# Router logits from raw rows, the last two tiles written out, and an earlier first list in a decoder layer

## The reference

```
x = x + xattn(layernorm(x), ctx)                      # the rows "x2"
xf = layernorm(x).reshape(2048, 256)                  # the rows "xn3"
route_prob = softmax(xf @ Ws + bs, axis=-1).T         # 8 x 2048
route_vals, routes = top_k(route_prob, 256)           # per expert
h   = gelu(xf[routes] @ W1[e] + b1[e])                # 256 x 1024
out = (h @ W2[e] + b2[e]) * route_vals
x   = x + scatter_add(out by routes)
```

## Time and profile before

| what | us |
|---|---|
| median of 3 runs | 368.83 |
| lowest, highest | 368.15, 371.8 |
| the profiled execution | 368.73 |
| its span, first to last instruction | 366.9 |
| TensorE busy | 321.4 (88%) |
| DVE busy | 281.0 (77%) |
| ScalarE busy | 189.2 (52%) |
| POOL busy | 195.0 (53%) |

### The profile page before, as it was taken

One profiled execution on the slowest core, in us unless ns is written; L12 is line 12 of the kernel. 1 busy time (PEld: TensorE's weight loads), 2 busy tenths in 40 slices (PEclk: granted clock), 3 DMA queues, 4 the chain that ended last, 5 costly groups with the idle time before them and its releaser, 6 DMA issues.

```text
span 366.9 us, 6429 instructions
## 1 busy us (share of the span) xinstructions
PE 321.4 (88%) x2346; PEld 289.8 (79%) x2346; DVE 281.0 (77%) x626; ACT 189.2 (52%) x370; POOL 195.0 (53%) x243
## 2 busy tenths in 40 slices
PE   8989998899979999999999982116999999999991
PEld 8867886675559999999999881106999999999991
DVE  2888888848877888888888846777578699689850
ACT  1677654446463467567755642682417556652230
POOL 3778789723142538887888783304314514543222
PEclk9999999999989999999999997555999999999997
DMA  7960000000000136134142346201148657611222
GB/s 234 378 226 1 2 0 2 0 0 3 0 2 0 42 117 188 34 126 136 66 144 79 122 146 185 116 0 31 57 155 249 173 213 189 172 19 41 30 30 29
DMA packets 24047, 34.29 MB, mean 93 GB/s; under 512 B 1784, under 2 KB 20560, under 8 KB 23888
## 3 DMA queue, kind: packets, MB, share of 16 engines
q1 hardware_dynamic: 20112, 29.36, 24.5%
q0 software_dynamic: 3072, 4.20, 6.5%
q10 hardware_dynamic: 832, 0.32, 0.4%
HBM read 27.58 MB, written 6.29 MB: 92 GB/s over the span
## 4 chain that ended last, share of the span: by engine, by line
PE 71%; DVE 13%; POOL 7%; ACT 4%; issue 3%; DMA 1%; DVEq 0%; POOLq 0%; ACTq 0%
PE bank L913 13%; PE bank L915 12%; PE bank L914 12%; PE q_banks L913 4%; PE bank L934 4%; PE q_banks L915 4%; PE q_banks L914 4%; PE bank L769 2%; DVE flags_all L1272 2%; PE q_banks L714 2%; PE bank L732 2%; PE bank L1448 2%; PE bank L748 2%; PE bank L978 1%; POOL acc L406 1%
## 5 line engine op out<-in xcount | busy, mean ns | idle before, releaser
L1573 POOL DMA_INDIRECT out_x<-ybuf,idx x16 | 26.1, 1629 | 59.8 <-DVE ybuf L1593 57.7
L1042 POOL TENSOR_TENSOR prob<-prob,rsum 128x1024 f32<-128x1024 f32 x16 | 30.5, 1906 | 18.8 <-DVE rsum L1140 17.4
L913 PE MATMUL bank<-H_hi,PT_hi 128*128 128x256 f32 x128 | 36.3, 284 | 1.7 <-DVE PT_lo L1111 1.7
L913 PE MATMUL bank<-W_hi,h_hi 128*128 128x256 f32 x128 | 37.2, 291 | 0.0
L915 PE MATMUL bank<-H_hi,PT_lo 128*128 128x256 f32 x128 | 36.2, 283 | 0.0
L915 PE MATMUL bank<-W_hi,h_lo 128*128 128x256 f32 x128 | 36.2, 283 | 0.0
L914 PE MATMUL bank<-H_lo,PT_hi 128*128 128x256 f32 x128 | 36.2, 283 | 0.0
L914 PE MATMUL bank<-W_lo,h_hi 128*128 128x256 f32 x128 | 36.2, 283 | 0.0
L1022 ACT ACTIVATE prob<-prob 128x1024 f32<-128x1024 f32 x16 | 16.9, 1059 | 34.8 <-DVE prob L1161 34.8
L1530 ACT ACTIVATE hbuf<-bank,b_cols 128x256 f32<-128x256 f32 x32 | 13.4, 471 | 40.1 <-PE bank L915 40.1
L1553 POOL DMA_INDIRECT xg<-xn_rows,idx x16 | 18.9, 1180 | 23.7 <-DVE idx L1621 19.4
(11 more groups left out here) (262 smaller groups left out, 1067.3 us busy)
## 6 DMA issues: line engine op xcount, KB each, us to landing
W_raw<-in_L_ffn_W SPq DMA_DIRECT2D x16, 1024.0 KB, 5.7
X<-in_x SPq DMA_DIRECT2D x4, 512.0 KB, 7.1
xn_rows<-xn SPq DMA_DIRECT2D x16, 128.0 KB, 1.8
out_x<-X SPq DMA_DIRECT2D x4, 512.0 KB, 3.6
Wq<-in_L_xattn_Wq SPq DMA_DIRECT2D x1, 1024.0 KB, 11.5
Wk<-in_L_xattn_Wk SPq DMA_DIRECT2D x1, 1024.0 KB, 14.1
Wv<-in_L_xattn_Wv SPq DMA_DIRECT2D x1, 1024.0 KB, 15.5
Wo<-in_L_xattn_Wo SPq DMA_DIRECT2D x1, 1024.0 KB, 16.9
```

The lines of the kernel that those rows point to most:

```text
L913: t.matmul(out_ps, hi, rhs_hi, start=first, stop=False)
L1042: g.tensor_tensor(prob[:, s], prob[:, s], rsum[:, s].unsqueeze(2).to_broadcast([P, HX, CK]), ALU.mult).then_inc(prob_ready, 1)
L1573: g.indirect_dma_start(out_flat, bass.IndirectOffsetOnAxis(ap=idx[:, e, h:h + 1], axis=0), ybuf[:, h], None, bounds_check=last_row, oob_is ...
```

## The change

- The router's logits are made from the transposed rows x2 themselves and from Ws less its columns' means. The means come in part 1: a tile mean_of of 1/256, two matmuls behind the "cols" transposes, a copy by ScalarE, a subtraction by DVE; ws_sb is loaded earlier. x2 of tile k-1 is transposed in step k. The factor rstd3 (now kept for all 16 tiles) is applied to the logits by DVE.
- The loop ends with step 13. The last two tiles are written out for each engine (`pe_drain`, `act_drain`, `pool_drain`, `dve_drain`). Tile 15's probabilities are scaled half by POOL, half by DVE; its product goes to bank 0; xn3 of tiles 14 and 15 is made by POOL; the softmax is taken over the first 14 tiles, in PSUM (`some`, in bank 1), and over each of the last two alone.
- POOL's second weight half of the drain comes last. SP sends the last output rows and loads W2 of expert 3 ahead of the last two xn3 tiles. POOL's iotas wait for the stored xn3 tiles instead of out_full.
- The first list's one-hot is made in three parts, and its list is read ahead of the second one-hot.

```diff
+            g.memset(mean_of[:], 1.0 / D)
             order(g.memset(ident[:], 0.0))
...
+            pe.wait_ge(ld["ws"], 16)
+            for m in range(MC):
+                mm = t.matmul(ps[:, P:P + E], mean_of[:], ws_sb[:, m], start=m == 0, stop=m == MC - 1)
+            filled(mm, "cols")
...
+            dve.wait_ge(cols_ready, 3)
+            v.tensor_tensor(ws_sb[:], ws_sb[:], gate_mean[:].unsqueeze(1).to_broadcast([P, MC, E]),
+                            ALU.subtract).then_inc(gate_ready, 1)
...
-        STEPS = steps(-LEAD_T, NT + DONE)
+        LAST = NT - 1
+        STEPS = steps(-LEAD_T, LAST - 1)
...
+        def x2_transposes(pe, n):
+
+            pe.wait_ge(x2_ready, n + 1)
+            for m in range(MC):
+                mm = nc.tensor.transpose(banks[6][:, D + m * P:D + (m + 1) * P], X[:, n, m * P:(m + 1) * P], ident[:])
+            return mm
...
-                pe.wait_ge(*xn3_of(n))
+            if old.within(NT):
                 if not nxt.within(NT):
                     pe.wait_ge(xT_ready, NT)
-                for m in range(MC):
-                    mm = t.transpose(banks[6][:, D + m * P:D + (m + 1) * P], xn3[:, s, m * P:(m + 1) * P], ident[:])
+                mm = x2_transposes(pe, old.n)
...
+        def pe_drain(pe):
+
+            n = LAST - 1
+            pe.wait_ge(prob_ready, n + 1)
+            pe.wait_ge(PT_ready, 2 * n)
+            prob_transposes(n, 0)
+            prob_transposes(n, 1)
+            pe.wait_ge(xT_ready, NT)
+            x2_transposes(pe, n - 1).then_inc(T_full, 1)
+            logits_product(pe, n - 1)
+            pe.wait_ge(PT_ready, 2 * n + 1)
+            out_product(banks[7], n, range(4))
+            pe.wait_ge(PT_ready, 2 * n + 2)
+            pe.wait_ge(prob_ready, NT)
+            prob_transposes(LAST, 0)
+            pe.wait_ge(last_prob_ready, 1)
+            prob_transposes(LAST, 1)
+            out_product(banks[7], n, range(4, 8)).then_inc(out_full, 1)
+
+            pe.wait_ge(shifted, LAST)
+            pe.wait_ge(PT_ready, 2 * LAST + 1)
+            out_product(banks[0], LAST, range(4))
+            pe.wait_ge(PT_ready, 2 * LAST + 2)
+            x2_transposes(pe, n).then_inc(T_full, 1)
+            out_product(banks[0], LAST, range(4, 8)).then_inc(out_full, 1)
+            pe.wait_ge(shifted, NT)
+            logits_product(pe, n).then_inc(logits_full, 1)
+
+            x2_transposes(pe, LAST).then_inc(T_full, 1)
+            logits_product(pe, LAST).then_inc(logits_full, 1)
...
+        def act_drain(act):
+            a = nc.scalar
+            n = LAST - 1
+            PT_high(act, n)
+            x2T_evac(act, n - 1)
+            for nth in LAST_HALVES:
+                W_high(act, nth)
+            PT_high(act, LAST)
+            xn3_row(act, n - 1)
+            x2T_evac(act, n)
+            act.wait_ge(shifted3, 1)
+            a.activation(some, some, ACT.Exp).then_inc(exp3_ready, 1)
+            x2T_evac(act, LAST)
+            for i in (n, LAST):
+                act.wait_ge(shifted3, i - n + 2)
+                a.activation(logits[:, i], logits[:, i], ACT.Exp, bias=rowmax[:, i:i + 1],
+                             accum_out=rowsum[:, i:i + 1]).then_inc(exp3_ready, 1)
...
+        def row_scale(pool, n, order):
+
+            g = nc.gpsimd
+            s = n % 2
+            pool.wait_ge(var3_ready, n + 1)
+            order(g.tensor_tensor(rstd3[:, n:n + 1], mv3[:, s, 1:2], eps_col[:], ALU.add))
+            raised = g.tensor_tensor(rstd3[:, n:n + 1], rstd3[:, n:n + 1], neg_half[:, 0:1], ALU.pow)
+            raised.then_inc(rstd3_ready, 1)
+            order(g.tensor_tensor(nmean3[:, s:s + 1], mv3[:, s, 0:1], neg_one[:], ALU.mult))
+            pool.wait_ge(rstd3_ready, n + 1)
+            return g.tensor_tensor(nmean3[:, s:s + 1], nmean3[:, s:s + 1], rstd3[:, n:n + 1], ALU.mult)
...
+        def pool_drain(pool, order):
+            g = nc.gpsimd
+            n, s = LAST - 1, LAST % 2
+            pool.wait_ge(rsum_ready, NT)
+            g.tensor_tensor(prob[:, s, 0:HALF], prob[:, s, 0:HALF],
+                            rsum[:, s, 0:HALF].unsqueeze(2).to_broadcast([P, HALF, CK]), ALU.mult).then_inc(prob_ready, 1)
+            row_scale(pool, n - 1, order).then_inc(nmean3_ready, 1)
+            W_low(pool, LAST_HALVES[0])
+            pool.wait_ge(xn3_ready, n)
+            row_scale(pool, n, order).then_inc(nmean3_ready, 1)
+            row_scale(pool, LAST, order).then_inc(nmean3_ready, 1)
+            pool.wait_ge(nmean3_ready, NT)
+            for i in (n, LAST):
+                pool.wait_ge(xn3_stored, 16 * (i - 1) + 16)
+                g.tensor_scalar(xn3[:, i % 2], X[:, i, :], rstd3[:, i:i + 1], nmean3[:, i % 2:i % 2 + 1], ALU.mult,
+                                ALU.add).then_inc(last_xn3_ready, 1)
+            W_low(pool, LAST_HALVES[1])
...
+        def dve_drain(dve, order):
+            v = nc.vector
+            n, s = LAST - 1, LAST % 2
+
+            def row_moments(i):
+                order(v.bn_stats(stats3[:, i % 2], X[:, i, :]))
+                v.bn_aggr(mv3[:, i % 2], stats3[:, i % 2]).then_inc(var3_ready, 1)
+
+            raw_logits = v3(banks[7][:, D:D + (NT - 2) * E], NT - 2)
+            add_out(dve, n - 1, banks[7])
+            dve.wait_ge(exp_ready, NT)
+            order(v.tensor_reduce(sums[:, s], prob[:, s], AX.X, ALU.add))
+            v.reciprocal(rsum[:, s], sums[:, s]).then_inc(rsum_ready, 1)
+            PT_low(dve, n)
+            dve.wait_ge(rsum_ready, NT)
+            v.tensor_tensor(prob[:, s, HALF:], prob[:, s, HALF:], rsum[:, s, HALF:].unsqueeze(2).to_broadcast([P, HALF, CK]),
+                            ALU.mult).then_inc(last_prob_ready, 1)
+            row_moments(n - 1)
+            PT_low(dve, LAST)
+            add_out(dve, n, banks[7])
+            row_moments(n)
+
+            dve.wait_ge(nmean3_ready, n)
+            dve.wait_ge(ld["small"], 32)
+            order(v.tensor_tensor(some, raw_logits, rstd3[:, ROUTED].unsqueeze(2).to_broadcast([P, n, E]), ALU.mult))
+            order(v.tensor_tensor(some, some, bs_bc[:].unsqueeze(1).to_broadcast([P, n, E]), ALU.add))
+            order(v.tensor_reduce(rowmax[:, ROUTED], some, AX.X, ALU.max))
+            v.tensor_tensor(some, some, rowmax[:, ROUTED].unsqueeze(2).to_broadcast([P, n, E]),
+                            ALU.subtract).then_inc(shifted3, 1)
+            add_out(dve, LAST, banks[0])
+            row_moments(LAST)
+            for i in (n, LAST):
+                dve.wait_ge(logits_full, i - n + 1)
+                dve.wait_ge(rstd3_ready, i + 1)
+                order(v.scalar_tensor_tensor(out=logits[:, i], in0=logits_of(i), scalar=rstd3[:, i:i + 1], in1=bs_bc[:],
+                                             op0=ALU.mult, op1=ALU.add))
+                v.tensor_reduce(rowmax[:, i:i + 1], logits[:, i], AX.X, ALU.max, negate=True).then_inc(shifted3, 1)
+                if i == n:
+                    dve.wait_ge(exp3_ready, 1)
+                    order(v.tensor_reduce(rowsum[:, ROUTED], some, AX.X, ALU.add))
+                    order(v.reciprocal(rowsum[:, ROUTED], rowsum[:, ROUTED]))
+                    v.tensor_tensor(probs[:, :, ROUTED].rearrange("p e i -> p i e"), some,
+                                    rowsum[:, ROUTED].unsqueeze(2).to_broadcast([P, n, E]), ALU.mult)
+                dve.wait_ge(exp3_ready, i - n + 2)
+                order(v.reciprocal(rowsum[:, i:i + 1], rowsum[:, i:i + 1]))
+                ins = v.tensor_scalar(probs[:, :, i], logits[:, i], rowsum[:, i:i + 1], None, ALU.mult)
+            ins.then_inc(probs_ready, 1)
...
+            def rows_out(n):
+                sp.wait_ge(x2_ready, n + 1)
+                sp.dma_start(out_rows[:, n - NJ + 1:n + 1, :], X[:, n - NJ + 1:n + 1, :]).then_inc(x2_stored, 16)
+                sp.wait_ge(out_full, n + 1)
+                load_W2(sp, n // NJ)
+
             for n in range(NT):
+                if n == LAST - 1:
+                    rows_out(LAST)
...
             pool.wait_ge(x2_stored, 16 * NT // NJ)
-            pool.wait_ge(out_full, NT)
+            pool.wait_ge(xn3_stored, 16 * NT + 16)
...
+        FIRST_PARTS = (slice(0, NT // 2), slice(NT // 2, 3 * NT // 4), slice(3 * NT // 4, NT))
...
             onehot_of(FIRST_LISTS[0])
             split_vals_by_position(1)
+            read_list(FIRST_LISTS[0])
             onehot_of(FIRST_LISTS[1])
-            read_list(FIRST_LISTS[0])
```

More of the change, by code:

```diff
@@ L915, in product3, with prob_transposes, logits_of, logits_product @@
             return t.matmul(out_ps, lo, rhs_hi, start=False, stop=last_one)
+        def prob_transposes(n, g):
+            t = nc.tensor
+            flat = prob[:, n % 2].rearrange("p h k -> p (h k)")
+            for c in range(4):
+                o = (4 * g + c) * P
+                mm = t.transpose(banks[4 + g][:, c * P:(c + 1) * P], flat[:, o:o + P], ident[:])
+            mm.then_inc(PT_full, 1)
+        def x2_transposes(pe, n):
[3 more added lines that the diff above has]
```

(44 more changed lines are left out.)

184 lines of the change are left out of this document (72 added, 112 removed).

## The result

The changed kernel takes 367.23 us (median of 18 runs, 365.54 to 368.33); the kernel before, beside it, 369.61 (18 runs, 366.62 to 372.37). The ratio is 0.9939, 95% interval 0.9919 to 0.9959. Two more series gave 0.9887 (0.9836 to 0.9938) and 0.9968 (0.9944 to 0.9993). So it is faster, by about 0.6%; the intervals of these two do not overlap, so over the three series its size is known only as 0.3 to 1.1%. Forecast were 365.0 and a range of 363.7 to 366.7, so the time lies above the range. The profiled execution's span is 365.5 against 366.9.

The account below looks back on a forecast made before the run. TensorE was taken to bound the loop, and a serial chain between engines the drain up to 226.53. Gains of 4.4 less 0.59 gave 3.8; the list's 0.15 and the start's cancelled: 368.83 to 365.0, range 363.7 to 366.7.

Parts of the forecast that it names:

- The rule against it: DVE and POOL in drain and search: from a cast that cost 0.02, no exclusive wait on SBUF was assumed.
- The rival: DVE blocks beside POOL at two drain scalings, costing 0.3 to 1.2 us: 365.3 to 366.2; chance 0.2.
- The sign named for it: Holes in DVE's row beside POOL between 221 and 225 us would show DVE blocked by POOL.
- The two tiles written out: Drain, tiles 14 and 15: product 1.7 us sooner, parallel branches 2.06, softmax 0.6; opening transpose at 13.6.
- zero: The out_full of tile 13, at 208.56 us before the change, from which the drain's times are counted.
- the lock: A port pair DVE and POOL share exclusively; if it held, two drain scalings would lose 0.3 to 1.2 us.
- The loop: Tile steps up to 13: one more step with transposes and logits, 0.59 us more, no wait on x2.
- the slower rival: TensorE stalls on x2 in each of thirteen steps; at 0.5 a step, 371.5 us; chance 0.05.
- The start: Part 1: a memset ahead of ident delays TensorE's warm-up by 0.15 us; Ws lands near 14.
- The search: Behind the opening transpose: a serial ping-pong with unchanged length; late xn3 stores and iotas cost nothing.
- The lists: Behind the search: first list and gather about 0.8 us sooner, but only 0.15 won, bounds 0 and 0.5.
- the second list: Ahead of the first expert: starts 0.15 us later, with unread matmuls behind it until 256.2.

Follow-up runs that it names:

- e1: The changed kernel with POOL's last weight half waiting until tile 15's probabilities are scaled; 364.77 us, ratio 0.9846 to the kernel before.
- e2: The changed kernel with the logits of tiles 14 and 15 in PSUM instead of SBUF; 365.23 us, ratio 0.9873 to the kernel before.
- e4: The changed kernel with POOL's second drain weight half moved back between the moments of tiles 14 and 15; 365.42 us, ratio 0.9910 to the kernel before.
- e8: The changed kernel with POOL's last weight half made in two operations of 128x512 instead of one; 366.59 us, ratio 0.9948 to the kernel before.
- e7: The changed kernel with last logits and search thresholds in PSUM, old order of first lists, mean_of filled behind ident; 364.32 us, ratio 0.9871 to before.
- e9: Second series of the changed kernel with all four mends (logits, thresholds, list order, mean_of); 362.57 us, ratio 0.9869 to the kernel before.
- e5: The changed kernel with the search's thresholds copied once to PSUM; 366.99 us, ratio 0.9947 to the kernel before.
- after_again: The changed kernel, unaltered, in a second series; 365.84 us, ratio 0.9887 to the kernel before.
- after_third: The changed kernel, unaltered, in a third series; 367.46 us, ratio 0.9968 to the kernel before.

## Why the prediction was wrong, step by step
- **Where it started.** The forecast went from 368.83, the median of three runs; beside the changed kernel the old one took 369.61. So 0.8 of the 2.2 us between 365.0 and 367.23 is the starting point; a gain of 3.8 was forecast and 2.4 measured.
- **The rule against it.** Here it failed. I set an exclusive wait between DVE and POOL at 0.02 from one row, a cast beside an operation of the search, gave the other reading a chance of 0.2, and priced it at 0.3 to 1.2. Measured: 2.2 at the scaling, and up to 0.55 in the search; the lists' gather issue grew by 0.77 beside a one-hot. The rival's mechanism was right. The sign named for it, holes in DVE's row beside POOL, was the wrong one to look for: there was one long record. Its price was wrong because I placed POOL's xn3 rows (each taken at 0.74) beside the last scaling and the half behind it. The two rows took 1.10 together, so they were nearly over when the scaling started, and POOL was at the half at 222.09, 0.07 behind that start. A wait as long as one of POOL's operations has to be priced by the longest that can stand there. The Trainium skill (SBUF — State Buffer, "Who interferes with whom") says that the shared pair is held for the whole instruction while the other engine is blocked, and that a tensor_scalar can enter a mode that takes it. e1, e2, e4 and e8 agree with it, the cast's 0.02 does not.
- **The two tiles written out.** Right: tile 15's add 9.72 behind zero (forecast 9.8), POOL's half-tile 2.05 behind it (1.96), its length 1.04 (1.05), the product of tile 14 from 211.35, 2.57 (2.71). Where the lock is away (e1, e2, e7, e9), the transpose comes 3.79 to 3.82 behind the last add: forecast 3.8 (13.6 less 9.8). That the whole came out right to 0.02 is in part luck: DVE was free 1.01 behind tile 15's add, not 1.12, and the work up to tile 15's first small operation took 1.43, not 1.58, while tile 15's own chain to the transpose took some 1.35 where I had 1.13. The small operations were 0.15 to 0.23 each.
- **The loop.** Step 1 is 7.29 long where it was 6.72 (113.67 to 120.96, 113.77 to 120.49): +0.57 for 0.59. But the loop's end came only 0.22 later. The start had given 0.10; the other 0.25 went in steps 2 to 13, some 0.02 a step (7.32 for 7.35 in each from step 3 on). Why, I haven't tested. TensorE's waits there are those of the earlier trace rows and none on x2, so the slower rival fell:

```profile
PE bank L939 <- DVE H_lo L907: 1.3, 1, 1.3
PE bank L888 <- DVE H_lo L907: 1.0, 2, 0.6
PE bank L957 <- ACT x2T L1061: 0.8, 1, 0.8
```

  The third is in the drain, where DVE's low parts were awaited anyway.
- **The start.** Ident was 0.14 later, as forecast, but warm-up took 8.22 where it was 8.46, and TensorE's transposes began 0.10 earlier. Over the traces warm-up takes 7.78 to 8.92 with the same instructions; the 0.15 is drowned in that. Ws landed in 6.3 us, and nothing waited for it.
- **The search.** Forecast rigid, was 0.55 longer. The step that failed is the one that let the stores land near 230, POOL's iotas start then, and cost nothing. They started at 228.78, and the result was ready in time; but POOL's operations for vals moved beside other rounds and met them head-on. A cover has to be asked what it disturbs, not only whether it is long enough.
- **The lists.** Forecast -0.15, measured +0.25 in the first traces, and some +0.25 at the same clock. The failed term is the second list: I had it 0.15 later, it began 7.07 behind taken instead of 6.74, 0.33 later. The third part brought TensorE's end of the first list only from 5.74 to 5.63 behind taken, the second one-hot now waits for that and its reading (from 5.81, where it had been from 5.24), and the unread matmuls start behind it. The forecast also had no term for the clock, which in most traces of the new order rose after the transposes or among them.
- **The sum.** In the traces +0.22 - 1.78 - 0.46 + 0.55 + 0.25 - 0.18 = -1.4. Of the forecast's 3.8 the lock took 2.2 in the drain and 0.5 in the search, the lists 0.4 (0.15 not won, 0.25 lost), and the start, the loop and the tail gave some 0.7 more than forecast. The medians' 2.4 lies between the traces' difference and the forecast.

## What to carry to other kernels
Before putting a long operation "off" on POOL, list the DVE instructions that may run beside it: if one of them, however small, reads SBUF in a form that waits for POOL (here a tensor_scalar of 128x8, and operations with two inputs in SBUF) and lies on the path, it costs up to the whole of POOL's operation, and no idle-time view will show it, only a record too long for its shape. Place such an operation behind a semaphore of the path, cut it into pieces, or keep the small operand in PSUM. And a transfer or a list read sooner is worth only as much as what its engine's next work was waiting for it.

## What the runs showed of the hardware
- DVE's scaling of 128x8 with an SBUF input took 2.44 us beside a POOL operation of 2.34 that started 0.07 later, 1.37 beside one of half the size, and 0.23 with its input in PSUM. DVE's record started first and DVE was the one that waited; but at that moment POOL's row before the half was still running, to 222.13. In e4, where nothing followed the rows, the scaling took 0.47 and ended 0.03 behind them.
- In the search an operation with two SBUF inputs took 0.55 and 0.62 beside POOL's tensor_tensors of 128x128 and 0.42 beside its cast, 0.35 otherwise (changed kernel, first trace); with one of the two inputs in PSUM (e5) none was over 0.35.
- An indirect gather's issue on POOL took 2.10 where it began 0.32 behind the start of a one-hot of two bf16 inputs in SBUF, and 1.33 behind its end. It is not so beside every one-hot: the changed kernel's third and fourth issue, at 253.70 and 255.00, took 1.00 each though one-hots ran from 253.90 to 256.26. What decides is not shown.
- Executions of one kernel differ by up to 5.8 us (the kernel before, 366.62 to 372.37). A part of it is TensorE's granted clock, which fell at one place or another under the same instructions: in the first traces of before and after from 106 to 112 us, in after_again from 20 to 30, in after_third in neither. Stretches of after, then of after_again, then of after_third (length, busy PE, PEld, DVE, ACT, POOL, PEclk, DMA share, GB/s):

```profile
106.00:112.00 6.00, 6.00 (x31) 5.33 (x30) 3.69 (x7) 1.95 (x4) 2.60 (x2) 0.77 0.01 3
```

```profile
20.00:30.00 10.00, 8.72 (x38) 6.98 (x37) 8.28 (x17) 6.43 (x17) 7.50 (x7) 0.83 0.39 131
```

```profile
106.00:112.00 6.00, 6.00 (x43) 5.52 (x41) 4.76 (x10) 1.89 (x5) 2.60 (x2) 1.00 0.01 3
```

  The same stretch holds 31 matmuls of after and 43 of after_third. From step 0 to the last add the changed kernel took 113.22 with the fall at 106 (after) and 111.65 and 111.64 without it (after_again, after_third): 1.6 us, as much as most edits here are worth. That is why the stretches of the traces, and not the medians, carry the verdicts. A second such place is behind the search: the clock was full again 10.6 us behind taken in the kernel before and 16.6 in e8, and from the first matmul to the end e8 took 110.36 where the three traces of the changed kernel took 108.64 to 108.79.
